# A graph filter layer: its first product in three-part bf16 instead of fp32

## Chip, cores and metric

The kernel runs on one core of one Trainium2 chip. The metric is the time of one execution in device microseconds (us). Three runs of the kernel before took 5813.36, 5824.89 and 5824.14 us, median 5824.14 us.

## What is computed

12,500 nodes have 128 features each; 400,000 edges, sorted by their target, have a source node, a target node, 20 attributes and a weight. The layer is a message passing step with a pre-norm and a residual:

```python
h = jnp.maximum(_layernorm(x), 0.0) @ W_in2f.T
Wij = smu(edge_attr_20 @ W_f1.T + b_f1) @ W_f2.T + b_f2      # per edge
Wij = Wij * edge_weight[:, None]
agg = segment_sum(h[dst] * Wij, src)                          # 12,500 sums
x = x + smu(agg @ W_o1.T + b_o1) @ W_o2.T + b_o2
```

`smu(x)` is close to a gelu: it is computed as `gelu(s x)` plus a multiple of `x`. The names follow the kernel: it gathers `h` by `dst`, in which the edges are sorted, and sums by `src`, which is in no order.

## The kernel before

Edges are taken 128 at a time (a tile), four tiles to a **unit** of 512 edges and two units to a pair; there are 784 units. Every engine runs the same sequence of beats, one unit to a beat, with its own instruction stream written out by `step` functions: some beats are unrolled, most stand in loops of four. In beat n an engine works partly on unit n and partly on unit n-1.

For one unit:

- SP loads, once in two units, the attributes `attr` (20 rows x 1024 edges, fp32, with a row of ones for the bias), the targets `ends` and the window `win` of `h` (L440 to L455).
- PE: `filter1` multiplies the attributes by `w_f1` into `p_z` (L1129, one fp32 product of 128 rows x 512 columns, which the trace shows as two MATMUL records). ACT takes the gelu of it (L678), DVE adds the linear part into `act1` (`smu`, L921).
- PE: `rank` counts for each edge its place among edges of the same bucket (L1152, L1168 into `p_pos`); DVE turns that into row numbers (`places` L945, `row_idx` L956).
- PE: `targets` picks the rows of `h` by a one-hot product (12 bf16 products into `p_h`, L1146: `h` is held in three bf16 parts). ACT weighs them by the edge weight (`hg`, L689). `filter2` (4 fp32 products, 8 records, L1135) gives `p_w`. DVE multiplies the two into `msg` (L938).
- POOL scatters the unit's 512 messages to rows in DRAM with four indirect DMAs (L553), after it has waited for `row_idx`, the keys and `msg`.

The order of PE's beat n is `filter1(n)`, `bucket_sum`, `rank(n-1)`, `targets(n-1)`, `filter2(n-1)`. There is one bank `p_z`, so `filter1(n)` waits for `smu(n-1)`; `targets(n-1)` waits until ACT has emptied `p_h` of the unit before. DVE's beat n is the one-hot of a bucket (`seg_hot`, L971), `smu(n)`, `pick` (L925), `onehot` (L930), `places(n-1)`, the sum into `agg`, `row_idx` and `msg(n-1)`.

The units are done in ten rounds (112, 112, 112, 112, 112, 80, 60, 40, 28, 16 units). From round 1 on the beats also read back the buckets that the round before has scattered (`seg`, L466) and sum them on PE with fp32 products (`bucket_sum`, L1180). Round 0 has none of that; it holds the rest of the layer norm and of `h` and the zeroing of the buckets instead. A prologue before the first beat prepares the first nodes, row numbers and constants. After the last unit come 28 groups of the output layers.

Of the kernel before, what the change touches and what calls it, by code (L numbers as in the profile page):

```python
# [6 lines left out]
ALU = mybir.AluOpType  # L7
# [3 lines left out]
LANES = 128  # L11
TILES_U = 4
UNIT = LANES * TILES_U
# [3 lines left out]
BODY = 4  # L17
DEEP = 7
PARTS = 3
WINDOW = LANES  # L20
# [62 lines left out]
def build(nc, n_nodes, n_edges, n_real, F, R, t):  # L83
# [21 lines left out]
    real_tiles = -(-n_real // LANES)  # L105
    PREPS = 12
# [18 lines left out]
    ends16 = nc.dram_tensor("ends16", [1, n_edges], U16, kind="Internal")  # L125
    reach_dram = nc.dram_tensor("reach_dram", [chunks, CHUNK], F32, kind="Internal")
# [3 lines left out]
    with ctx:  # L130
# [22 lines left out]
        w_f1 = sb("w_f1", [LANES, F])  # L153
        w_f2 = sb("w_f2", [F, F])
# [32 lines left out]
        attr = sb("attr", [LANES, 2, PAIR])  # L187
# [30 lines left out]
        hid_lin = hg[:, :, :, :].rearrange("p b k f -> p b (k f)")[:, :, 0:GROUP]  # L218
        g_dst = sb("g_dst", [LANES, TILES_U], I32)
# [29 lines left out]
        s_limit, s_last = sem("s_limit"), sem("s_last")  # L249
        s_st, s_ag, s_sqrt, s_rstd, s_shift = sem("s_st"), sem("s_ag"), sem("s_sqrt"), sem("s_rstd"), sem("s_shift")  # L250
# [85 lines left out]
        class Beat:  # L336
# [26 lines left out]

            def q(self, back=0):
                return (self.c - back) // 2 % 2
# [41 lines left out]
        def _(sp):  # L407
# [8 lines left out]

            load_x(0)
            sp.dma_start(win_first[:, :], t["dst_first"]).then_inc(s_first, 16)
# [7 lines left out]
            sp.dma_start(w_f1[R:R + 1, :], t["b_f1"]).then_inc(s_ld, 16)  # L426
            for dst, src in ((w_f2[:, :], t["w_f2T"]), (w_o1[:, :], t["w_o1T"]), (w_o2[:, :], t["w_o2T"]),
                             (bias_o1[:, :], t["biases"][0, 1, :].unsqueeze(1)),
                             (bias_o2[:, :], t["biases"][0, 2, :].partition_broadcast(NODE_P))):
                sp.dma_start(dst, src).then_inc(s_ld, 16)  # L430
            for g in range(H_AHEAD):
# [72 lines left out]
            def everywhere():  # L504
                sp.wait_ge(s_z, n_units)
                sp.wait_ge(s_ph, n_units)
                with sp.Fori(0, n_units) as u:
                    sp.wait_ge(g_msg, u)
                    sp.sem_inc(s_carry, 1)
                    sp.dma_start(attr[0:R, 0, 0:UNIT], t["attrT"][:, bass.ds(u * UNIT, UNIT)]).then_inc(g_ld, 16)  # L510
# [9 lines left out]
        def _(pool):  # L520
            pool.memset(w_f1[:, :], 0.0).then_inc(s_pool, 1)
# [789 lines left out]
```

## Time and profile before

| | |
|---|---|
| median of 3 runs | 5824.14 us |
| the profiled execution | 5816.75 us |
| its span, first to last instruction | 5815.0 us |
| mean granted TensorE clock | 0.824 of 2.4 GHz |
| PE, PEld busy | 4372.5, 3583.8 us |
| DVE, ACT, POOL busy | 3423.3, 2117.0, 3038.9 us |
| DMA | 736.96 MB, mean 127 GB/s |

The page gives busy times over the whole span. The kernel has 784 equal beats, so a busy time divided by 784 is that of a beat, and 5815.0 / 784 = 7.42 us is the time there is for one, prologue and end included. In timelines "idle before" stands in square brackets with what ended it; `remote` means that the profile found no instruction of this core whose end fits.

### The profile page before, as it was taken

The numbers are of one execution on the slowest core, as the hardware profiler recorded it, in microseconds if no ns is written. First come the engines' busy times: TensorE is split into PE (matmuls) and PEld (weight loads), VectorE is DVE, ScalarE is ACT, GpSimd is POOL, SyncE is SP. The second block draws the span as 40 slices with busy tenths as digits, with TensorE's granted clock in tenths as the row PEclk, the third lists the DMA queues.
The fourth block names the chain that finished last, engine by engine and source line by source line (L and its number), as shares of the span: only waits on it lengthen the run. The fifth ranks groups of instructions, "written<-read, shape, count | busy, mean of one in ns | idle before, by whom it ended". The sixth has DMA issues, their size and how long they took to land.

```text
span 5815.0 us, 115644 instructions
## 1 busy us (share of the span) xinstructions
PE 4372.5 (75%) x32414; PEld 3583.8 (62%) x32414; DVE 3423.3 (59%) x11901; ACT 2117.0 (36%) x7301; POOL 3038.9 (52%) x3173
## 2 busy tenths in 40 slices
PE   5666557777777777777777777777777788888888
PEld 4455445666666666666666666666666666666667
DVE  5556445555565555555555655555665666666667
ACT  3455333333333333333333333333333333333332
POOL 4555555555555555555555555555555555555552
PEclk7777777877888887888888888888898888888889
DMA  5344334444443333334344434333444444444557
GB/s 161 108 133 135 110 105 131 131 130 130 130 122 113 112 112 115 116 112 115 110 113 115 120 113 114 109 112 117 124 136 134 133 143 142 134 139 145 155 145 196
DMA packets 460268, 736.96 MB, mean 127 GB/s; under 512 B 87920, under 2 KB 256218, under 8 KB 459856
## 3 DMA queue, kind: packets, MB, share of 16 engines
q1 hardware_dynamic: 292886, 461.84, 29.5%
q0 software_dynamic: 100000, 206.60, 10.6%
q10 hardware_dynamic: 67098, 65.08, 3.4%
q8 instruction: 136, 2.23, 0.2%
q14 instruction: 148, 1.21, 0.1%
HBM read 465.36 MB, written 267.82 MB: 126 GB/s over the span
## 4 chain that ended last, share of the span: by engine, by line
another core or an unknown queue 35%; PE 31%; issue 13%; DVE 9%; ACT 8%; ACTq 2%; DMA 1%; DVEq 1%; SPq 0%
PE p_seg L1180 8%; PE p_w L1135 7%; PE p_z L1129 7%; PE p_h L1146 7%; ACT hg L689 4%; DVE product L945 2%; ACT p_w L703 1%; PE p_pos L1152 1%; DVE seg_hot L971 1%; DVE onehot L930 1%; PE p_pos L1168 1%; DVE act L921 1%; ACT gelu L678 1%; ACTq L651 1%
## 5 line engine op out<-in xcount | busy, mean ns | idle before, releaser
L553 POOL DMA_INDIRECT sorted_rows<-msg,row_idx x3125 | 2997.8, 959 | 2685.0 <-DVE msg L938 1759.0
L689 ACT ACTIVATE hg<-p_h,weight 128x128 f32<-128x128 f32 x3136 | 894.6, 369 | 3163.3 <-remote 2888.8
L1180 PEld LDWEIGHTS p_seg<-seg_hot,seg 128*128 128x128 f32 x8288 | 1229.6, 215 | 818.9 <-issue 815.6
L945 DVE CUSTOM_DVE_ANT_0 product<-onehot,p_pos,start_at 128x112 bf16<-128x112 bf16 x3136 | 848.4, 327 | 1419.6 <-remote 1378.6
L1180 PE MATMUL p_seg<-seg_hot,seg 128*128 128x112 f32 x8288 | 1301.9, 300 | 353.9 <-issue 325.1
L1135 PE MATMUL p_w<-w_f,act 128*128 128x128 f32 x6272 | 1148.4, 327 | 238.6 <-issue 235.9
L1129 PE MATMUL p_z<-attr,w_f 128*128 128x512 f32 x1568 | 999.1, 715 | 192.4 <-issue 106.8
L1135 PEld LDWEIGHTS p_w<-w_f,act 128*128 128x128 f32 x6272 | 987.0, 233 | 247.7 <-issue 245.9
L1146 PE MATMUL p_h<-win,pick 128*128 128x128 bf16 x9408 | 831.4, 250 | 297.9 <-ACT hg L689 242.7
L938 DVE TENSOR_TENSOR msg<-p_w,hg 128x512 f32<-128x512 f32 x784 | 541.1, 690 | 757.5 <-ACT hg L689 512.3
L1146 PEld LDWEIGHTS p_h<-win,pick 128*128 128x128 bf16 x9408 | 701.7, 114 | 334.4 <-issue 333.5
L678 ACT ACTIVATE gelu<-p_z 128x512 f32<-128x512 f32 x784 | 474.0, 605 | 409.5 <-PE p_z L1129 160.0
L921 DVE SCALAR_TENSOR_TENSOR act<-p_z,gelu 128x512 f32<-128x512 f32 x784 | 539.0, 688 | 142.7 <-issue 93.2
L971 DVE SCALAR_TENSOR_TENSOR seg_hot<-seg,p_iota 128x560 f32<-128x560 f32 (+3 forms) x756 | 589.9, 787 | 11.2 <-DMA seg<-sorted_rows 7.5
L1152 PE MATMUL p_pos<-onehot,not_before 128*128 128x112 bf16 x3136 | 338.2, 234 | 259.2 <-DVE place L945 137.4
L1152 PEld LDWEIGHTS p_pos<-onehot,not_before 128*128 128x128 bf16 x3136 | 258.4, 111 | 410.4 <-issue 397.3
L930 DVE TENSOR_TENSOR onehot<-p_iota,node_l 128x448 bf16<-128x448 f32 x784 | 482.5, 615 | 0.0
L703 ACT COPY p_w<-bias_f 128x512 f32<-128x512 f32 x784 | 477.8, 609 | 0.0
L1129 PEld LDWEIGHTS p_z<-attr,w_f 128*128 128x128 f32 x1568 | 297.9, 228 | 288.5 <-issue 206.7
L1168 PE MATMUL p_pos<-onehot,before 128*128 128x112 bf16 x3136 | 336.6, 237 | 31.3 <-issue 31.2
L925 DVE TENSOR_SCALAR pick<-ends,win_row 128x512 bf16<-128x512 uint16 x784 | 297.6, 380 | 0.0
L945 DVE DVE_READ_ACCUMULATOR2_ANT place<- 128x1 f32 x3136 | 265.1, 85 | 0.0
(109 smaller groups left out, 1706.7 us busy)
## 6 DMA issues: line engine op xcount, KB each, us to landing
seg<-sorted_rows SPq DMA_DIRECT2D x560, 322.5 KB
ends<-ends SPq DMA_DIRECT2D x392, 256.0 KB
seg<-sorted_rows SPq DMA_DIRECT2D x112, 516.0 KB
sorted_rows<-msg,row_idx POOLq DMA_INDIRECT x3125
sorted_rows<-zero_rows ACTq DMA_DIRECT2D x336, 129.0 KB
win<-h SPq DMA_DIRECT2D x392, 96.0 KB
attr<-in_attrT SPq DMA_DIRECT2D x392, 80.0 KB
seg<-sorted_rows SPq DMA_DIRECT2D x56, 387.0 KB
```

The source lines that it names most:

```text
L553: pool.indirect_dma_start(out=sorted_rows[:, :], out_offset=bass.IndirectOffsetOnAxis(ap=row_idx[:, slot, k:k + 1], axis=0), in_=msg[:, sl ...
L689: last = act.activation(hg[:, v, k, :], p_h[:, k, :], ACT.Copy, scale=weight[:, bass.ds(n.value(TILES_U, k), 1)])
L921: dve.scalar_tensor_tensor(act1[:, v, :], p_z[:, :], SMU_L, gelu[:, v, :], ALU.mult, ALU.add).then_inc(s_smu, 1)
L930: dve.tensor_tensor(onehot[:, slot, :, :], p_iota[:, 0:BUCKETS].unsqueeze(1).to_broadcast([LANES, TILES_U, BUCKETS]), node_l[:, bass.ds(n. ...
L938: dve.tensor_tensor(msg[:, slot, :, 0:F], p_w[v][:, :, :], hg[:, v, :, :], ALU.mult).then_inc(s_msg, 1)
L945: last = dve.tensor_tensor_reduce(out=product[:, k, :], in0=onehot[:, slot, k, :], in1=p_pos[:, 0:BUCKETS], scale=1.0, scalar=start_at[:, ...
L971: dve.scalar_tensor_tensor(seg_hot[:, it.slot, 0:n, :], seg[:, it.slot, 0:n, F:F + 1].to_broadcast([LANES, n, NODE_P]), -float(LANES * (it ...
L1129: pe.matmul(p_z[:, :], w_f1[:, :], attr[:, q, v * UNIT:(v + 1) * UNIT], start=True, stop=True).then_inc(s_z, 1)
L1135: last = pe.matmul(p_w[v][:, k, :], act1[:, v, k * LANES:(k + 1) * LANES], w_f2[:, :], start=False, stop=(k == TILES_U - 1), skip_group_ch ...
L1146: last = pe.matmul(p_h[:, k, :], pick[:, v, k * LANES:(k + 1) * LANES], win[:, q, part * F:(part + 1) * F], start=(part == 0), stop=(part ...
L1152: last = pe.matmul(p_pos[:, 0:BUCKETS], not_before[:, :], onehot[:, slot, k, :], start=False, stop=False, skip_group_check=True)
L1180: last = pe.matmul(out, seg[:, it.slot, l * it.tiles + k, 0:F], seg_hot[:, it.slot, l * it.tiles + k, :], start=(k == 0), stop=(k == it.ti ...
```

## The change

Attributes and first-layer weights (with their bias) are each split into three bf16 parts that add up to the fp32 value. The weights are split once, in the prologue, on DVE, and laid out by 12 small DMAs into `w_z` (128 rows: part 0 three times 20 rows against the three attribute parts, part 1 the same, and the three parts of the bias on rows of ones) and `w_z3` (64 rows: part 2 against the three attribute parts). `filter1` becomes two accumulating bf16 products of 512 columns.

The attributes are split on the chip for each **quad** of four units: SP loads `raw` (80 rows x 512, fp32), ACT casts it (`part_one`), DVE subtracts (`part_rest`), ACT casts the rest (`part_two`), DVE subtracts again (`part_three`), and SP stores the three parts to a DRAM tensor `attr3` in four DMAs. `load_pair` then loads the pair's 60 rows x 1024 bf16 from there twice, into two groups of rows of `attr`. A quad is split two quads ahead of its use.

```diff
-                sp.dma_start(attr[0:R, q, :], t["attrT"][:, bass.ds(p.value() * PAIR, PAIR)]).then_inc(s_attr[q], 16)
+                if p.i is None and p.base % 2 == 0:
+                    sp.wait_ge(s_written, 16 * QUAD * (p.base // 2 + 1))
+                elif p.i is not None and p.base % 2 == 0:
+                    wait_for(sp, s_written, p.over(2), 16 * QUAD, 16 * QUAD)
+                    sp.sem_inc(s_carry, 1)
+                for twin in range(2):
+                    sp.dma_start(attr[twin * PARTS * R:(twin + 1) * PARTS * R, q, :],
+                                 attr3[bass.ds(p.value(PARTS * R), PARTS * R), :]).then_inc(s_attr[q], 16)
...
+            def load_raw(q):
+                wait_for(sp, s_rest, q)
+                sp.sem_inc(s_carry, 1)
+                sp.dma_start(raw[:, :], t["attr_quad"][bass.ds(q.value() * split_rows, split_rows), :]).then_inc(s_raw, 16)
+
+            def store_parts(q):
+                wait_for(sp, s_part3, q, 1, 1)
+                sp.sem_inc(s_carry, 1)
+                for k in range(QUAD):
...
+                    sp.dma_start(rows.rearrange("(a r) e -> r a e", r=R), part[k * R:(k + 1) * R, :, :]).then_inc(s_written, 16)
...
+                if st.quad(1, 1) is not None:
+                    store_parts(st.quad(1, 1))
+                if st.quad(1) is not None:
+                    load_raw(st.quad(1))
...
+            def part_one(q):
+                wait_for(act, s_raw, q, 16, 16)
+                wait_for(act, s_written, q, 16 * QUAD)
+                act.copy(part[:, 0, :], raw[:, :]).then_inc(s_part1, 1)
+
+            def part_two(q):
+                wait_for(act, s_rest, q, 1, 1)
+                act.copy(part[:, 1, :], rest[:, :]).then_inc(s_part2, 1)
...
+                if st.quad(0) is not None:
+                    part_one(st.quad(0))
+                if st.quad(1) is not None:
+                    part_two(st.quad(1))
...
+            def part_rest(q):
+                wait_for(dve, s_part1, q, 1, 1)
+                wait_for(dve, s_part3, q)
+                dve.tensor_tensor(rest[:, :], raw[:, :], part[:, 0, :], ALU.subtract).then_inc(s_rest, 1)
+
+            def part_three(q):
+                wait_for(dve, s_part2, q, 1, 1)
+                dve.tensor_tensor(part[:, 2, :], rest[:, :], part[:, 1, :], ALU.subtract).then_inc(s_part3, 1)
...
+                if st.quad(1) is not None:
+                    part_rest(st.quad(1))
+                if st.quad(2) is not None:
+                    part_three(st.quad(2))
...
-                    wait_for(pe, s_attr[q], p.over(2), 16, 16)
+                    wait_for(pe, s_attr[q], p.over(2), 32, 32)
                 wait_for(pe, s_smu, n)
-                pe.matmul(p_z[:, :], w_f1[:, :], attr[:, q, v * UNIT:(v + 1) * UNIT], start=True, stop=True).then_inc(s_z, 1)
+                cols = slice(v * UNIT, (v + 1) * UNIT)
+                pe.matmul(p_z[:, :], w_z[:, :], attr[:, q, cols], start=True, stop=False)
+                pe.matmul(p_z[:, :], w_z3[:, :], attr[0:LANES // 2, q, cols], start=False, stop=True).then_inc(s_z, 1)
```

`quad(phase)` is true in one beat of four, the one whose number leaves `phase`. The prologue gets the splits of quads 0 and 1, the split of the weights, and a wait of PE for `s_wz`.

How the streams change. **DVE**, an unrolled beat of a round with bucket sums in the kernel before, around `msg` and `smu` (the rows of `places` left out at both ends; `s_hg`, `s_w` are the ends of ACT's weighing and of `filter2`):

```order
L956 TENSOR_TENSOR row_idx<-place,place_max 128x4 [waits s_scat1,s_place]
L938 TENSOR_TENSOR msg<-p_w,hg 128x4x128 [waits s_scat1,s_w,s_hg]
L971 SCALAR_TENSOR_TENSOR seg_hot<-seg,p_iota 128x560 [waits s_seg,s_segld0]
L921 SCALAR_TENSOR_TENSOR act<-p_z,gelu 128x512 [waits s_w,s_gelu]
L925 TENSOR_SCALAR pick<-ends,win_row 128x512 [waits s_ph]
L930 TENSOR_TENSOR onehot<-p_iota,node_l 128x448 [waits s_rank]
```

and the same place with the change, in a beat that splits:

```order
L1054 TENSOR_TENSOR row_idx<-place,place_max 128x4 [waits s_scat0,s_place]
L1036 TENSOR_TENSOR msg<-p_w,hg 128x4x128 [waits s_scat0,s_w,s_hg]
L1069 SCALAR_TENSOR_TENSOR seg_hot<-seg,p_iota 128x560 [waits s_seg,s_segld1,s_ends1]
L963 TENSOR_TENSOR part<-rest,part 80x512 [waits s_part2]
L1019 SCALAR_TENSOR_TENSOR act<-p_z,gelu 128x512 [waits s_w,s_gelu]
L1023 TENSOR_SCALAR pick<-ends,win_row 128x512 [waits s_ph]
L1028 TENSOR_TENSOR onehot<-p_iota,node_l 128x448 [waits s_rank]
```

The subtraction stands between a message and the next `smu`, never ahead of the message itself; in the beat before it L959 stands at the same place.

**SP**, one quad of the steady part with the change (`attr` in rows L453 is the DRAM tensor `attr3`):

```order
L521 DMA seg<-sorted_rows 128x645 [waits s_seg] x2
L453 DMA attr<-part 20x3x512 [waits s_part3]
L453 DMA attr<-part 20x3x512 x3
L445 DMA raw<-in_attr_quad 80x512 [waits s_rest]
L521 DMA seg<-sorted_rows 128x645 [waits s_seg]
L495 DMA attr<-attr 60x1024 [waits s_z]
L495 DMA attr<-attr 60x1024
L501 DMA ends<-ends 128x1024 [waits s_pick]
```

Before, the three `seg` loads, one `attr` load and the `ends` load followed each other; four stores, `raw` and a second `attr` load are put between them.

**PE**, end of the prologue, before:

```order
L1106 MATMUL p_seg<-w_in,hT 128x128 x3
L1122 MATMUL p_w<-bias_f,ident 128x128 [waits s_seeds,s_pool,s_pool2,s_scaled]
L1122 MATMUL p_w<-bias_f,ident 128x128 x7
L1129 MATMUL p_z<-attr,w_f 128x512 [waits s_attr0]
L1129 MATMUL p_z<-attr,w_f 128x512 [waits s_smu]
```

and with the change:

```order
L1209 MATMUL p_seg<-w_in,hT 128x128 x3
L1226 MATMUL p_w<-bias_f,ident 128x128 [waits s_pool,s_seeds,s_wz,s_pool2,s_scaled]
L1226 MATMUL p_w<-bias_f,ident 128x128 x7
L1234 MATMUL p_z<-attr,w_z 128x512 [waits s_attr0]
L1235 MATMUL p_z<-attr,w_z 128x512
L1234 MATMUL p_z<-attr,w_z 128x512 [waits s_smu]
L1235 MATMUL p_z<-attr,w_z 128x512
```

PE's first products now also wait for the laid-out weights, and `p_z` takes two instructions.

## Rows read from the trace of the kernel before

**Rows 1.** Page, part 5: line engine op out<-in xcount | busy, mean ns | idle before, releaser.
```profile
L553 POOL DMA_INDIRECT sorted_rows<-msg,row_idx x3125 | 2997.8, 959 | 2685.0 <-DVE msg L938 1759.0
L689 ACT ACTIVATE hg<-p_h,weight 128x128 f32<-128x128 f32 x3136 | 894.6, 369 | 3163.3 <-remote 2888.8
L1129 PE MATMUL p_z<-attr,w_f 128*128 128x512 f32 x1568 | 999.1, 715 | 192.4 <-issue 106.8
```
**Rows 2.** Busy time by stretch: late round 0, round 1 and 2, rounds 6 and 7.
```profile
core 0: us, PE busy (x) PEld busy (x) DVE busy (x) ACT busy (x) POOL busy (x), PEclk, DMA share, GB/s
620.00:800.00 180.00, 107.79 (x772) 82.32 (x770) 86.37 (x329) 65.01 (x228) 96.82 (x101) 0.74 0.36 107
1000.00:1600.00 600.00, 462.39 (x3301) 376.33 (x3302) 341.72 (x1194) 213.49 (x755) 314.86 (x329) 0.80 0.44 130
4700.00:5300.00 600.00, 489.37 (x3791) 410.90 (x3790) 372.68 (x1257) 212.19 (x753) 320.85 (x334) 0.87 0.47 139
```
**Rows 3.** Timeline, 2021 to 2038 us, some rows: start, us, instruction [idle before <-releaser].
```profile
2021.04 0.96 POOL L553 DMA_INDIRECT sorted_rows<-msg,row_idx  x1 [0.31 <-issue]
...
2023.63 0.33 DVE L945 CUSTOM_DVE_ANT_0 product<-onehot,p_pos,start_at 128x112 bf16<-128x112 bf16 x1 [6.00 <-remote]
2023.94 1.14 ACT L689 ACTIVATE hg<-p_h,weight 128x128 f32<-128x128 f32 x4 [7.92 <-remote]
...
2025.12 0.69 DVE L938 TENSOR_TENSOR msg<-p_w,hg 128x512 f32<-128x512 f32 x1
...
2025.33 0.61 ACT L703 COPY p_w<-bias_f 128x512 f32<-128x512 f32 x1
...
2025.73 0.73 DVE L971 SCALAR_TENSOR_TENSOR seg_hot<-seg,p_iota 128x560 f32<-128x560 f32 x1
2025.85 0.62 ACT L678 ACTIVATE gelu<-p_z 128x512 f32<-128x512 f32 x1
2026.50 0.69 DVE L921 SCALAR_TENSOR_TENSOR act<-p_z,gelu 128x512 f32<-128x512 f32 x1
2026.71 0.96 POOL L553 DMA_INDIRECT sorted_rows<-msg,row_idx  x1 [4.72 <-DVE msg L938]
...
2028.57 1.02 PE L1129 MATMUL p_z<-attr,w_f 128*128 128x512 f32 x2
...
2029.24 0.69 DVE L938 TENSOR_TENSOR msg<-p_w,hg 128x512 f32<-128x512 f32 x1
2029.43 1.26 PE L1180 MATMUL p_seg<-seg_hot,seg 128*128 128x112 f32 x10
...
2030.93 0.83 PE L1146 MATMUL p_h<-win,pick 128*128 128x128 bf16 x12
...
2035.55 0.96 POOL L553 DMA_INDIRECT sorted_rows<-msg,row_idx  x1 [0.30 <-issue]
...
2038.31 1.14 ACT L689 ACTIVATE hg<-p_h,weight 128x128 f32<-128x128 f32 x4 [8.08 <-remote]
```
**Rows 4.** Timeline near the end of round 9, where POOL has run dry.
```profile
5690.24 0.83 PE L1146 MATMUL p_h<-win,pick 128*128 128x128 bf16 x12
...
5691.12 1.14 ACT L689 ACTIVATE hg<-p_h,weight 128x128 f32<-128x128 f32 x4 [3.91 <-PE p_h L1146]
...
5694.46 0.83 PE L1146 MATMUL p_h<-win,pick 128*128 128x128 bf16 x12
...
5695.33 1.14 ACT L689 ACTIVATE hg<-p_h,weight 128x128 f32<-128x128 f32 x4 [2.22 <-PE p_h L1146]
```
**Rows 5.** Timeline of the prologue.
```profile
21.43 0.22 DVE L897 TENSOR_SCALAR w_f<-w_f 128x128 f32<-128x128 f32 x1
...
29.25 0.69 DVE L834 TENSOR_TENSOR h_parts<-h_rest,h_parts 128x512 bf16<-128x512 f32 x1 [0.68 <-ACT h_parts L642]
...
30.59 3.75 PE L1122 MATMUL p_w<-bias_f,ident 128*128 128x128 f32 x16 [3.37 <-DVE seeds L905]
```
**Rows 6.** POOL alone, a unit that is scattered alone.
```profile
3021.56 0.96 POOL L553 DMA_INDIRECT sorted_rows<-msg,row_idx  x1 [0.30 <-issue]
3025.16 0.96 POOL L553 DMA_INDIRECT sorted_rows<-msg,row_idx  x1 [2.64 <-DVE msg L938]
```

More of the change, by code:

```diff
@@ L19 @@
 PARTS = 3
+QUAD = 4
+LEAD = 2
 WINDOW = LANES
@@ L105, in build @@
     real_tiles = -(-n_real // LANES)
+    n_quads = n_units // QUAD
+    assert n_units % QUAD == 0 and 2 * PARTS * R + PARTS <= LANES
+    split_rows = QUAD * R
     PREPS = 12
@@ L153, in build @@
         w_f1 = sb("w_f1", [LANES, F])
+        w_rest = sb("w_rest", [R + 1, F])
+        w_part = sb("w_part", [R + 1, PARTS, F], BF16)
+        w_z = sb("w_z", [LANES, F], BF16)
+        w_z3 = sb("w_z3", [LANES // 2, F], BF16)
         w_f2 = sb("w_f2", [F, F])
@@ L185, in build @@
         counts = sb("counts", [1, rounds + 1, BUCKETS])
-        attr = sb("attr", [LANES, 2, PAIR])
+        attr = sb("attr", [LANES, 2, PAIR], BF16)
+        raw = sb("raw", [split_rows, UNIT])
+        rest = sb("rest", [split_rows, UNIT])
+        part = sb("part", [split_rows, PARTS, UNIT], BF16)
         ends = sb("ends", [LANES, 2, PAIR], U16)
@@ L218, in build @@
         hid_lin = hg[:, :, :, :].rearrange("p b k f -> p b (k f)")[:, :, 0:GROUP]
+        g_attr = gelu[:, 1, :]
         g_dst = sb("g_dst", [LANES, TILES_U], I32)
@@ L249, in build @@
         s_limit, s_last = sem("s_limit"), sem("s_last")
+        s_raw, s_part1, s_rest, s_part2, s_part3, s_w3 = (
+            sem(n) for n in ("s_raw", "s_part1", "s_rest", "s_part2", "s_part3", "s_w3"))
+        s_written = sem("s_written")
+        s_wz, s_wpart, s_wzero = sem("s_wz"), sem("s_wpart"), sem("s_wzero")
         s_st, s_ag, s_sqrt, s_rstd, s_shift = sem("s_st"), sem("s_ag"), sem("s_sqrt"), sem("s_rstd"), sem("s_shift")
@@ L362, in chunk, with quad @@
                 return self.first(back) // CHUNK if self.i is None and self.has(back) and self.first(back) % CHUNK == 0 else None
+            def quad(self, phase, back=0):
+                if self.c % QUAD != phase or self.rnd >= rounds:
+                    return None
+                at = Count((starts[self.rnd] + self.c) // QUAD + LEAD - back, BODY // QUAD if self.i is not None else 0, self.i)
+                return at if self.i is not None or at.base < n_quads else None
             def q(self, back=0):
@@ L430, in _ @@
                 sp.dma_start(dst, src).then_inc(s_ld, 16)
+            sp.wait_ge(s_wpart, 1)
+            sp.wait_ge(s_wzero, 1)
+            for k in range(2 * PARTS):
+                sp.dma_start(w_z[k * R:(k + 1) * R, :], w_part[0:R, k // PARTS, :]).then_inc(s_wz, 16)
+            for k in range(PARTS):
+                sp.dma_start(w_z3[k * R:(k + 1) * R, :], w_part[0:R, 2, :]).then_inc(s_wz, 16)
+                sp.dma_start(w_z[2 * PARTS * R + k:2 * PARTS * R + k + 1, :], w_part[R:R + 1, k, :]).then_inc(s_wz, 16)
+            store_parts(Count(0))
             for g in range(H_AHEAD):
@@ L894, in _ @@
             dve.wait_ge(s_ld, 16 * N_LD)
+            part_three(Count(0))
+            dve.tensor_copy(w_rest[:, :], w_f1[0:R + 1, :]).then_inc(s_w3, 1)
+            dve.wait_ge(s_w3, 1)
+            for k in range(PARTS - 1):
+                link(dve.tensor_copy(w_part[:, k, :], w_rest[:, :]))
+                link(dve.tensor_tensor(w_rest[:, :], w_rest[:, :], w_part[:, k, :], ALU.subtract))
+            dve.tensor_copy(w_part[:, PARTS - 1, :], w_rest[:, :]).then_inc(s_wpart, 1)
             dve.tensor_scalar(bias_gelu[:, :], bias_o1[:, :], SMU_S, None, ALU.mult)
@@ L901, in _ @@
                 third_part(g)
+            part_rest(Count(1))
+            part_three(Count(1))
             dve.wait_ge(s_pool, 4)
@@ L1231, in everywhere @@
                     pe.wait_ge(g_ld, u * 32 + 32)
-                    pe.matmul(p_z[:, :], w_f1[:, :], attr[:, 0, 0:UNIT], start=True, stop=True).then_inc(g_z, 1)
+                    pe.matmul(p_z[:, :], w_f1[:, :], g_attr[:, :], start=True, stop=True).then_inc(g_z, 1)
                     pe.wait_ge(g_win, u * (16 * TILES_U) + 16 * TILES_U)
```

18 lines of the change are left out of this document (17 added, 1 removed).

## The prediction

> **What bounds the kernel now.** I read the page's costliest groups first. They mislead: PE is busy 75% of the span, yet two idle times are larger than any work. ACT waits 2888.8 us for `remote` ahead of weighing `p_h`, and POOL waits 1759.0 us for messages [rows 1]. A bound by PE would show PE full and the others waiting for it in varying amounts, so I then asked for the pace of the beats in stretches with different PE work. Four scatters make a unit. In late round 0 there are 101 scatters in 180 us, 7.13 us per unit; PE has no bucket sums there and is busy 107.79 / 25.25 = 4.27 us per unit. In rounds 1 and 2 it is 7.29 us per unit with PE at 5.62 us, in rounds 6 and 7 7.19 us with PE at 5.86 us [rows 2]. So 1.35 to 1.59 us more PE work per unit costs 0.06 to 0.16 us, and DVE's work grows in the same stretches (3.42, 4.15, 4.46 us) as freely. Traffic of 107, 130 or 139 GB/s makes no difference either. Only POOL is the same everywhere.
>
> The timeline says how [rows 3]. POOL works in bursts of eight scatters, 1.26 us apart (0.96 busy, 0.30 issue), 10.1 us in all. While such a burst runs, PE's ends come late: the 12 products into `p_h` are recorded at 2030.93 for 0.83 us, but ACT, which needs nothing else, weighs them only at 2038.31, for `remote`. The last scatter of that burst ended at 2035.55 + 0.96 = 2036.51, 1.8 us earlier. One cycle back it is the same: last scatter until 2022.00, DVE goes on at 2023.63 and ACT at 2023.94. Where POOL has run dry, `p_h` of 5690.24 is weighed at 5691.12 and that of 5694.46 at 5695.33, right after its end, and the beat takes 4.2 us though it has 32 bucket records [rows 4]. What holds PE's ends back I can't see; that they come free 1.6 to 1.9 us after a burst I can. From that the cycle follows: release at 2023.9, `hg` 1.14 us, `msg` 0.69 us until 2025.81, POOL 0.90 us later at 2026.71; the second unit's message is ready before the first unit's four scatters are done, so POOL runs eight; release again. 10.1 + 1.8 + 2.8 = 14.7 us less 0.3 us of the last issue gap, 14.4 us for two units, 7.2 us each.
>
> **PE's part of the change.** Removed: 784 fp32 products of 512 columns. A record is 715 ns in the mean and busy time is 999.1 us [rows 1]; back to back the pair holds the array for 2029.43 - 2028.57 = 0.86 us at the full clock [rows 3]. Added: two bf16 products of 512 columns. The 12 of 128 columns into `p_h` take 0.83 us, of which the last one's drain is a good part, so 0.05 to 0.07 us each [rows 3]; four times the columns are 0.22 to 0.28 us, 0.43 to 0.55 us for the pair. The array is relieved of 0.3 to 0.4 us per unit at 2.4 GHz, up to twice that at 1.2 GHz: 240 to 630 us in all. On the path I cost it at **0**. `filter1(n)` ends inside the stretch in which nothing that PE ends is seen, or ahead of it; its cover is POOL's burst. The message that starts a burst hangs on the `p_h` and `p_w` of the unit before, which stand ahead of the next `filter1` in PE's order. The slope of rows 2 gives the other end: 0.16 us per 1.35 us, times 0.4 to 0.8 us, times 784, is -37 to -74 us.
>
> The Trainium skill, "FP8 and Floating Point Precision", section "TensorE Precision Notes", says that a true fp32 product takes four passes of the array. By that rule this product falls from four passes to two; the trace agrees (0.86 us against two times 0.22 us), and a kernel whose path ran through PE would gain that. It is the first rival below that it would make true.
>
> **DVE and ACT.** Added per quad: two subtractions of 80 x 512 fp32. `smu`, of the same width, takes 0.69 us [rows 3]; so 1.38 us per quad. ACT: two casts of 80 x 512, like the copy of 0.61 us [rows 3]. Both lie between a message and the next `smu`; the message that starts POOL is not behind them. The second message of a burst is: after the release DVE goes `msg`, `seg_hot` until 2026.46, `smu` at 2026.50, and ACT the copy until 2025.94, `gelu` until 2026.47. A cast (0.61) and then a subtraction (0.69), with `gelu` beside the latter, move this `smu` by 0.7 us and the message of 2029.24 with it. It ended at 2029.93 and POOL needs it at 2026.71 + 4 x 1.26 - 0.90 = 30.85 on this scale, so there is **0.9 us of slack**. Each quad has two such beats, and where a split falls into the other beat of a cycle it lies in the wait. Mostly the slack holds; I allow one cycle in four a loss of 0.1 us or so, 392 / 4 x 0.1 = **10 us**. Bounds: nothing, and 0.7 us in every second cycle, 137 us.
>
> **SP and DMA.** Per quad SP issues 1 raw load, 4 stores and 2 more attribute loads, 7 DMAs. SP is three beats ahead of the others, and every new wait (`s_part3`, `s_rest`, `s_written`) is for work of a beat that lies at least two back, so **0**. Queued behind them are `seg`, `ends` and `win`, for beats later. Bytes: 160 + 240 + 480 KB instead of 160 KB per quad, 720 KB x 196 = 141 MB, 19% more than 737 MB. Rows 2 show the same pace from 107 to 139 GB/s: **0**. The other end: if a quad's 720 KB stood on the path at some 300 GB/s, 2.4 us x 196 = 470 us.
>
> **Prologue.** DVE gets two subtractions ahead of the first `h` parts (1.4 us), the split of the weights, six small operations that wait for each other (0.22 us each as the scaling at 21.43, with the waits about 1.5 us), and the split of quad 1 (two more subtractions with ACT's casts between, 2.6 us) between its last `h_parts` at 29.25 and the `seeds` for which PE's `p_w` products of 30.59 wait [rows 5]. SP's 12 small DMAs and 4 stores run beside that. About **+5 us**, bounds 2 and 12. The end of the kernel is not touched.
>
> **Sum** on the profiled execution: 5816.75 - 0 + 10 + 0 + 5 = 5832. The median of the runs is 7.4 us above that execution, so 5839; I say **5838 us**, +0.24%. A measurement of this kernel tells about 0.2%, 11.6 us, from no change.
>
> **Rivals.** *A, PE's work counts (the other side).* The late ends could be PE's own backlog: it works through products that are queued, and the coincidence with POOL follows from POOL waiting for PE. Then 0.43 us per unit, 337 us, give 5490; at half that share, with the cycle partly POOL's, 5660; by the slope of rows 2 5750 to 5790. Against: rounds without bucket sums are no faster. It decides from the point where a third unit passes PE before the ends are held, or where the first message comes earlier. For a small gain, something speaks: the cold clock after a release (the clock is 0.74 to 0.87 in rows 2, so part of the time at 1.2 GHz) makes that beat's products slow.
>
> *B, the split costs a burst.* If the second message comes after POOL's fourth scatter by more than a moment, PE's ends of the unit behind are caught too and POOL scatters four alone. Such a unit is seen: its last scatter starts at 3021.56 and the next burst at 3025.16, 5.05 + 2.3 = 7.4 us for one unit instead of 7.2 [rows 6]. In half the cycles, that is 0.2 x 392 = 78 us; with the 0.7 us delays on top, 5824 + 78 + 70 = 5970. It decides where the slack is under 0.7 us.
>
> *C, the change does not arrive:* the attributes make a round trip through DRAM, and if stores or the second load are late, `filter1` waits for `s_attr` once a quad. At 1 us, 5824 + 196 = 6020. Against: two quads of lead.
>
> **How the numbers follow.** The forecast, pace unchanged with 2 to 30 us of small costs, has 0.50; with the rounding of measurement half of it lies within 0.2%, half above. A has 0.30, mostly its small form. B has 0.15, C 0.05. So faster 0.29, same 0.28, slower 0.43. The range: 5740, the slope's gain, to 5920, most of B; about 0.1 is left out on each side.
>
> **What would show it.** Right: POOL's scatters still in eights with 4.6 us between, `remote` ahead of `hg` still near 2900 us, PE's busy time down by 400 us or more, pace of rows 2 unchanged, first `gelu` 5 us later. Wrong: `remote` falls by hundreds of us with PE's busy time (A), more bursts of four (B), or PE waits for DMA ahead of `p_z` (C).

## The result, and the profile after

| | before | changed |
|---|---|---|
| median of the runs | 5822.62 us (4) | 5874.93 us (4) |
| the profiled execution, its span | 5816.75, 5815.0 us | 5860.67, 5858.8 us |
| ratio | | 1.0092, 95% interval 1.0078 to 1.0105 |
| PE, DVE, ACT, POOL busy | 4372.5, 3423.3, 2117.0, 3038.9 us | 4302.2, 3659.3, 2307.9, 3118.8 us |
| granted clock, mean | 0.824 | 0.797 |
| DMA | 736.96 MB | 881.68 MB |

The change costs 52 us, 0.9%. I had forecast a loss of 14 us. The page's groups, to be held against [rows 1] (line, engine, op, out<-in, count | busy, mean ns | idle before, releaser):

```profile
L615 POOL DMA_INDIRECT sorted_rows<-msg,row_idx x3125 | 3077.5, 985 | 2650.2 <-DVE msg L1036 1718.9
L764 ACT ACTIVATE hg<-p_h,weight 128x128 f32<-128x128 f32 x3136 | 896.0, 369 | 3182.4 <-remote 2833.0
L1286 PE MATMUL p_seg<-seg_hot,seg 128*128 128x112 f32 x8288 | 1415.0, 320 | 339.8 <-issue 318.1
...
L1234 PE MATMUL p_z<-attr,w_z 128*128 128x512 bf16 x784 | 348.3, 444 | 234.6 <-issue 137.0
...
L1235 PE MATMUL p_z<-attr,w_z 64*128 64x512 bf16 x784 | 343.1, 438 | 84.1 <-issue 82.7
```

The first filter's group fell by 308 us (999.1 to 348.3 + 343.1), and nothing of it arrived. POOL's 3125 scatters are the same instructions with the same bytes, yet they take 79.7 us more. The three stretches of [rows 2] in the changed kernel:

```profile
core 0: us, PE busy (x) PEld busy (x) DVE busy (x) ACT busy (x) POOL busy (x), PEclk, DMA share, GB/s
620.00:800.00 180.00, 102.59 (x758) 79.94 (x759) 93.17 (x340) 69.60 (x238) 100.27 (x101) 0.70 0.47 131
1000.00:1600.00 600.00, 445.43 (x3295) 364.84 (x3292) 362.27 (x1227) 228.15 (x778) 326.98 (x330) 0.79 0.54 155
4700.00:5300.00 600.00, 472.24 (x3710) 397.05 (x3710) 392.95 (x1283) 228.80 (x779) 323.73 (x331) 0.83 0.56 163
```

The number of scatters per stretch is as before (101, 330, 331 against 101, 329, 334), but POOL's busy time for each scatter is up, by 3.6, 3.5 and 1.8%. So the pace nearly holds and the scatters themselves grew. The timeline shows how, in the place that answers to [rows 3]:

```profile
2012.52 0.69 DVE L1036 TENSOR_TENSOR msg<-p_w,hg 128x512 f32<-128x512 f32 x1
...
2013.13 0.73 DVE L1069 SCALAR_TENSOR_TENSOR seg_hot<-seg,p_iota 128x560 f32<-128x560 f32 x1
2014.00 0.69 DVE L959 TENSOR_TENSOR rest<-raw,part 80x512 f32<-80x512 f32 x1
2014.12 1.55 POOL L615 DMA_INDIRECT sorted_rows<-msg,row_idx  x1 [4.79 <-DVE msg L1036]
...
2015.97 0.96 POOL L615 DMA_INDIRECT sorted_rows<-msg,row_idx  x1 [0.30 <-issue]
...
2028.83 0.96 POOL L615 DMA_INDIRECT sorted_rows<-msg,row_idx  x1 [4.32 <-DVE msg L1036]
```

The scatter begins 0.12 us after the new subtraction, which ends at 2014.69; it takes 1.55 us, that is the 0.57 us until then plus its usual 0.96. The next one and the first of the next burst take 0.96 again. There are 176 scatters of 1100 ns and more, against 7 before.

From here on I divide every span along POOL, since it is the engine that all of them follow. The rows are sums over its 3125 scatters and the times between them, in us; gaps under 0.6 us are issue gaps, longer ones are waits.

| profiled execution | to first scatter | scatters | issue gaps | waits | after the last | span |
|---|---|---|---|---|---|---|
| before | 45.9 | 2997.8 | 813.5 | 1831.5 | 126.3 | 5815.0 |
| changed | 56.4 | 3077.5 | 816.3 | 1783.8 | 124.8 | 5858.8 |
| before_again | 47.6 | 2998.6 | 814.4 | 1840.2 | 123.8 | 5824.6 |
| after_again | 60.2 | 3078.0 | 817.5 | 1778.5 | 126.3 | 5860.3 |
| split_alone | 56.3 | 3078.3 | 822.7 | 1772.4 | 126.3 | 5855.9 |
| *other chips:* no_split | 55.1 | 3000.3 | 952.0 | 13.2 | 124.6 | 4145.1 |
| before_psum | 48.1 | 3012.8 | 951.7 | 8.0 | 124.1 | 4144.8 |
| before_port_b | 47.6 | 3053.0 | 951.1 | 13.4 | 123.9 | 4189.0 |
| pool_delay | 45.3 | 3006.7 | 892.6 | 133.0 | 124.1 | 4201.5 |
| one_input_b | 55.9 | 3017.3 | 950.6 | 21.7 | 123.7 | 4169.3 |
| after_c | 57.1 | 3051.5 | 951.7 | 17.0 | 125.3 | 4202.7 |
| late | 56.4 | 3052.6 | 947.9 | 33.0 | 125.0 | 4214.9 |

Changed less before: +10.5 for the start, +79.7 for the scatters, +2.8 issue, -47.7 waits, -1.5 at the end: 43.8 us, the whole difference of the two spans.

**Two kinds of chip.** The experiments met four chips. On one the kernel before takes 5822 us as above; on the three others 4137.46, 4138.23 and 4137.51 us. Which chip the result itself was measured on isn't known; its 5822.62 us put it with the first kind. Whether it is the chip that differs, or something else that came with it, no run shows. A number is only compared with the kernel before as timed beside it on the same chip; on the 4138 us chips the kernel before was timed and not profiled. What differs is in the table's fifth column: on the other three POOL hardly ever waits (8 to 33 us; the 133 us of pool_delay hold its own added work). The `hg` group of after_c there, and the timeline of before_port_b:

```profile
L764 ACT ACTIVATE hg<-p_h,weight 128x128 f32<-128x128 f32 x3136 | 891.6, 367 | 662.3 <-PE p_h L1252 618.5
```
```profile
2094.67 0.95 POOL L556 DMA_INDIRECT sorted_rows<-msg,row_idx  x1 [0.30 <-issue]
...
2095.49 0.83 PE L1153 MATMUL p_h<-win,pick 128*128 128x128 bf16 x12
...
2096.55 1.14 ACT L692 ACTIVATE hg<-p_h,weight 128x128 f32<-128x128 f32 x4 [0.44 <-PE p_h L1153]
2097.19 0.96 POOL L556 DMA_INDIRECT sorted_rows<-msg,row_idx  x1 [0.30 <-issue]
```

Here `hg` follows its products by 0.23 us in the middle of unbroken scatters, where [rows 3] had it wait 6.6 us for `remote`. These chips are the plainer instrument: every us on POOL is a us of the kernel, 3125 x (0.96 + 0.305) us = 3953 of 4138.

### The profile page after: what moved, and what is told of

The parts are those of the page before. It is cut to its first block, busy times and chain, and to the rows that moved or that the text cites. A ratio compares the mean times of both kernels' runs of the same rounds, so it can differ in the third digit from the quotient of the medians.

```text
span 5858.8 us, 120689 instructions
## 1 busy us (share of the span) xinstructions
PE 4302.2 (73%) x32414; PEld 3541.6 (60%) x32414; DVE 3659.3 (62%) x12299; ACT 2307.9 (39%) x7693; POOL 3118.8 (53%) x3175
## 2 busy tenths in 40 slices
DMA packets 581381, 881.68 MB, mean 150 GB/s; under 512 B 107102, under 2 KB 322440, under 8 KB 580958
## 3 DMA queue, kind: packets, MB, share of 16 engines
q0 software_dynamic: 100000, 206.60, 10.5%
## 4 chain that ended last, share of the span: by engine, by line
another core or an unknown queue 31%; PE 31%; issue 14%; ACT 12%; DVE 6%; ACTq 2%; DMA 1%; SPq 0%; DVEq 0%
PE p_seg L1286 10%; PE p_h L1252 7%; PE p_w L1241 7%; ACT hg L764 4%; PE p_z L1235 2%; ACT p_w L778 2%; PE p_z L1234 2%; ACT gelu L753 2%; PE p_pos L1258 1%; DVE product L1043 1%; PE p_pos L1274 1%; ACTq L713 1%; DVE seg_hot L1069 1%; DVE onehot L1028 1%
## 5 line engine op out<-in xcount | busy, mean ns | idle before, releaser
L615 POOL DMA_INDIRECT sorted_rows<-msg,row_idx x3125 | 3077.5, 985 | 2650.2 <-DVE msg L1036 1718.9
L1286 PE MATMUL p_seg<-seg_hot,seg 128*128 128x112 f32 x8288 | 1415.0, 320 | 339.8 <-issue 318.1
L1241 PE MATMUL p_w<-w_f,act 128*128 128x128 f32 x6272 | 1177.2, 336 | 211.9 <-issue 208.6
L1241 PEld LDWEIGHTS p_w<-w_f,act 128*128 128x128 f32 x6272 | 1022.3, 242 | 215.1 <-issue 213.5
L1252 PE MATMUL p_h<-win,pick 128*128 128x128 bf16 x9408 | 870.6, 258 | 284.8 <-ACT hg L764 248.6
L1252 PEld LDWEIGHTS p_h<-win,pick 128*128 128x128 bf16 x9408 | 741.4, 119 | 318.3 <-issue 317.5
L1019 DVE SCALAR_TENSOR_TENSOR act<-p_z,gelu 128x512 f32<-128x512 f32 x784 | 534.7, 682 | 93.6 <-issue 69.3
L1234 PE MATMUL p_z<-attr,w_z 128*128 128x512 bf16 x784 | 348.3, 444 | 234.6 <-issue 137.0
L1235 PE MATMUL p_z<-attr,w_z 64*128 64x512 bf16 x784 | 343.1, 438 | 84.1 <-issue 82.7
L1274 PE MATMUL p_pos<-onehot,before 128*128 128x112 bf16 x3136 | 351.5, 244 | 62.4 <-issue 62.3
L1235 PEld LDWEIGHTS p_z<-attr,w_z 64*128 64x128 bf16 x784 | 73.9, 94 | 387.5 <-issue 387.5
L1023 DVE TENSOR_SCALAR pick<-ends,win_row 128x512 bf16<-128x512 uint16 x784 | 295.0, 376 | 0.0
```

Of the source, the lines that this page charges most:

```text
L615: pool.indirect_dma_start(out=sorted_rows[:, :], out_offset=bass.IndirectOffsetOnAxis(ap=row_idx[:, slot, k:k + 1], axis=0), in_=msg[:, sl ...
L1241: last = pe.matmul(p_w[v][:, k, :], act1[:, v, k * LANES:(k + 1) * LANES], w_f2[:, :], start=False, stop=(k == TILES_U - 1), skip_group_ch ...
L1252: last = pe.matmul(p_h[:, k, :], pick[:, v, k * LANES:(k + 1) * LANES], win[:, q, part * F:(part + 1) * F], start=(part == 0), stop=(part ...
L1286: last = pe.matmul(out, seg[:, it.slot, l * it.tiles + k, 0:F], seg_hot[:, it.slot, l * it.tiles + k, :], start=(k == 0), stop=(k == it.ti ...
```

## The experiments

The theories: **port** (a scatter that begins while DVE reads two operands from SBUF is held until it ends), with the start-up beside it; against **TensorE** (the product's relief or its clock), **bytes** (145 MB more) and **slack** (DVE's added time makes the messages late).

**On the kind of chip of the result.** The two kernels again, and the changed one with the fp32 product and the loads of before, which splits and stores without anybody reading it:

```diff
-                for twin in range(2):
-                    sp.dma_start(attr[twin * PARTS * R:(twin + 1) * PARTS * R, q, :],
-                                 attr3[bass.ds(p.value(PARTS * R), PARTS * R), :]).then_inc(s_attr[q], 16)
+                sp.dma_start(attr[0:R, q, :], t["attrT"][:, bass.ds(p.value() * PAIR, PAIR)]).then_inc(s_attr[q], 16)
...
-                pe.matmul(p_z[:, :], w_z[:, :], attr[:, q, cols], start=True, stop=False)
-                pe.matmul(p_z[:, :], w_z3[:, :], attr[0:LANES // 2, q, cols], start=False, stop=True).then_inc(s_z, 1)
+                pe.matmul(p_z[:, :], w_f1[:, :], attr[:, q, cols], start=True, stop=True).then_inc(s_z, 1)
```

> The kernel before, for a profile of it on the chip of the experiments: 4137 us, scatters of 959 ns as on the first chip (busy 2998 us), none of the waits that the first chip's trace put down as remote, start-up as on the first chip (first gelu at 37 us).

> The changed kernel itself on the chip of the experiments, where the kernel before takes 4137 us and not 5823 us. There GpSimd waits for a message only 78 us in all beside its issue gaps, so its busy time is the time: the port theory expects busy near 3078 us as on the first chip and the kernel at +80 +8 us, about 4225 us (ratio 1.021). If the 48 us that GpSimd waited less on the first chip come back here too, 4180 us. TensorE theory (two bf16 products instead of one fp32 product are the gain): not above 4137 us.

> The changed kernel with the fp32 product and the attribute loads of before; it still splits and stores the parts, which nobody reads back. Port theory: the same as the changed kernel within 10 us, with long scatters as many. Bytes theory: some 60% of the added cost, since of the added 145 MB the stores and the quad loads stay and the double loads are gone. TensorE theory: slower than the changed kernel by 100 us and more, since the first filter's product is back at 715 ns a piece of four passes.

Measured: these runs met the 5822 us chip, so the numbers that were expected for the other kind of chip weren't tried by it. Before 5822.09 us; after_again 5863.12 us, 1.0081 [1.0067, 1.0095]; split_alone 5853.94 us, 1.0055 [1.0042, 1.0069]. The groups of split_alone:

```profile
L609 POOL DMA_INDIRECT sorted_rows<-msg,row_idx x3125 | 3078.3, 985 | 2645.1 <-DVE msg L1030 1714.3
L1228 PE MATMUL p_z<-attr,w_f 128*128 128x512 f32 x1568 | 989.8, 707 | 249.8 <-issue 168.6
```

The heavy product is back, 989.8 against 350.3 + 344.8 us in after_again, and the kernel is no slower; it is 9 us faster, with one load where there were two. So TensorE's relief gains nothing here, and the split with its start-up carries 32 of the 41 us. What the other 9 us belong to, the second load or the two-part product, isn't separated. The long scatters are all there (173 of 1100 ns and more), and so is the shorter wait (1772.4), which therefore doesn't come from the lighter product.

**The hold, alone.** The kernel before with two subtractions per quad that nobody waits for; then the same with the second operand in PSUM:

```diff
+                if st.has() and st.c % 4 in (1, 2):
+                    dve.tensor_tensor(rest[:, st.c % 4 - 1, :], raw[:, :], part[:, :], ALU.subtract)
```
```diff
+                if st.has() and st.c % 4 in (1, 2):
+                    dve.tensor_tensor(rest[:, st.c % 4 - 1, :], raw[:, :], p_iota[0:4 * R, :], ALU.subtract)
```

> The kernel before with two VectorE subtractions per quad added, of the changed kernel's size and types (80 x 512, fp32 minus bf16, both operands in SBUF), at the same place in the beat, that nobody waits for. No transfer, no ScalarE work, no TensorE work is changed. Port theory: the long first scatters appear here too, some 160 to 200 of them, GpSimd's busy time rises by 70 to 90 us and the kernel by 30 to 80 us over the one before. Bytes theory: no change (within 10 us). Slack theory: also slower, but with scatters of their old length and more GpSimd idle time.

> The kernel before with two VectorE subtractions per quad, both operands in SBUF, that nobody waits for, a second time; it may meet the other chip. Port theory: some 130 to 180 scatters that begin while one of these subtractions runs take 1100 ns and more, GpSimd's busy time is 55 to 80 us above 2998. Where GpSimd never waits (4137 us chip) that is the whole cost, +46 us as before; where it stands idle between bursts (5822 us chip) part of it comes back, as it did in the changed kernel: +20 to +45 us.

> The same two subtractions, their second operand in PSUM (fp32) instead of SBUF (bf16). Port theory: none of the scatters that begin beside them is held (mean 957 to 970 ns), GpSimd's busy time at most 20 us above 2998, the kernel at +0 to +20 us. If it is not the port but VectorE's time that costs: the same time as with both operands in SBUF, within 5 us.

Measured, all on 4138 us chips: before_port 4183.47 us, 1.0112 [1.0096, 1.0127]; before_port_b 4185.97 us, 1.0115 [1.0099, 1.013]; before_psum 4150.18 us, 1.0032 [1.002, 1.0044]. Timelines of before_port_b and before_psum, the same place in the beat:

```profile
2107.21 0.68 DVE L999 TENSOR_TENSOR rest<-raw,part 80x512 f32<-80x512 f32 x1
2107.30 1.42 POOL L556 DMA_INDIRECT sorted_rows<-msg,row_idx  x1 [0.30 <-issue]
```
```profile
2087.84 0.68 DVE L998 TENSOR_TENSOR rest<-raw,p_iota 80x512 f32<-80x512 f32 x1
2087.95 0.96 POOL L555 DMA_INDIRECT sorted_rows<-msg,row_idx  x1 [0.30 <-issue]
```

Same engine, size, duration and offset (0.09 and 0.11 us); one scatter is held, the other isn't. Scatters sorted by what DVE was executing 0.1 us after they began (count, mean ns, of them over 1050 ns; the smaller groups are left out):

| DVE at that moment | inputs | count | mean | long |
|---|---|---|---|---|
| changed kernel: `rest` L959 | two SBUF | 140 | 1373 | 117 |
| changed kernel: third part L963 | two SBUF | 143 | 1105 | 57 |
| changed kernel: `smu` L1019 | SBUF, PSUM | 401 | 962 | 6 |
| changed kernel: `pick` L1023 | one SBUF, 16-bit in and out | 146 | 974 | 8 |
| changed kernel: `product`, `onehot`, `seg_hot`, `msg`, `agg` | SBUF, PSUM | 424, 317, 161, 149, 75 | 958 or 959 | 0 |
| changed kernel: nothing | | 989 | 958 | 0 |
| before_port_b: subtraction | two SBUF | 180 | 1222 | 138 |
| before_psum: subtraction | SBUF, PSUM | 192 | 959 | 1 |
| before_psum: `pick` L929 | one SBUF, 16-bit in and out | 186 | 1018 | 62 |

Which of the two begins first decides. Of the scatters that begin 0.05 to 0.4 us after a subtraction with two SBUF operands every one is over 1050 ns: 162 of 162 in the changed kernel, 114 of 114 in before_port_b, 97 of 97 in after_c. With the PSUM operand it is 1 of 120 in before_psum and 1 of 102 in one_input_b. Of the 100 in the changed kernel that begin up to 0.1 us ahead of the subtraction none is; 82 of them are among the 143 beside the third part, whence the low share there. The two versions of the subtraction also differ in the type of the second operand (bf16 in SBUF, fp32 in PSUM). A bf16 operand from SBUF alone doesn't hold a scatter: `product` reads bf16 `onehot` from SBUF beside `p_pos` in PSUM, and none of its 424 is long. Two fp32 operands in SBUF weren't tried.

The Trainium skill, "SBUF — State Buffer", section "Who interferes with whom", has this rule: a DVE instruction with two SBUF inputs contends with a GpSimd instruction that reads SBUF, one with at most one outside the 2-port modes doesn't, and `tensor_scalar` can be in such a mode. The table agrees in each line, `pick`'s too, if the scatter is taken for an instruction that reads SBUF. The DVE instructions of 0.6 us and more that stand in every beat of the kernel before take one operand from PSUM (`p_iota`, `p_z`, `p_w`), and only 7 of its scatters reach 1100 ns; six of these stand beside index operations that are done seven times in all (L852, L854, L872).

Bytes aren't needed for it: no transfer was added here, and 46 to 48 us came. Slack isn't it either: the same DVE time costs 12 us with a PSUM operand. These 12 us look like scatters as well (3012.8 against 3000.3 us in no_split, another kernel on another of these chips): 62 are long beside `pick` there, 18 in no_split. before_port had 150 scatters of 1100 ns and more and POOL some 57 us busier than the kernel before of the first table, where 160 to 200 and 70 to 90 us had been expected; the sizes were too high, the sign and the place right.

**The hold without its cause.** An idle iota on POOL ahead of one unit in four:

```diff
+                if held:
+                    wait_for(pool, s_idle, n.over(4))
+                    pool.sem_inc(s_go, 1)
+                    pool.iota(idle[:, :], pattern=[[1, 392]], base=0, channel_multiplier=0,
+                              allow_small_or_imprecise_dtypes=True).then_inc(s_idle, 1)
```

> The kernel before with one iota of some 0.37 us on GpSimd ahead of the scatters of one unit in four: 196 of them, 73 us, and with their fixed part some 80 to 100 us, at no cost to VectorE or to anything else. It is the hold of the changed kernel without its cause. Where GpSimd never waits, all of it is added: +80 to +100 us. Where it idles between bursts: if a hold ahead of a burst gives TensorE time that the wait after the burst then returns (as the changed kernel's 80 us and its 48 us less idle suggest), +30 to +50 us; if the less idle time came from elsewhere (the lighter product, VectorE's order), +80 us and more here too.

Measured on a 4138 us chip: 4203.28 us, 1.0161 [1.0147, 1.0175].

```profile
L560 POOL DMA_INDIRECT sorted_rows<-msg,row_idx x3125 | 3006.7, 962 | 933.5 <-issue 861.2
```

A gap with an iota takes 0.635 us in the mean in place of 0.305, 65 us for 196 of them; 65 us arrive. I had expected 80 to 100: the iota takes 0.45 us, but it begins 0.01 us after the scatter ahead of it ends, inside what was the issue gap. POOL's delay is paid in full on such a chip. On the 5822 us chip this kernel wasn't run, so what a delay costs there stands on the traces alone, below.

**Parts of the change.** First all but the split within the loop; then the changed kernel with PSUM operands; then with the subtractions moved:

```diff
-                if self.c % QUAD != phase or self.rnd >= rounds:
+                if True:
                     return None
...
-                                 attr3[bass.ds(p.value(PARTS * R), PARTS * R), :]).then_inc(s_attr[q], 16)
+                                 attr3[0:PARTS * R, :]).then_inc(s_attr[q], 16)
```
```diff
-                dve.tensor_tensor(rest[:, :], raw[:, :], part[:, 0, :], ALU.subtract).then_inc(s_rest, 1)
+                dve.tensor_tensor(rest[:, :], raw[:, :], p_iota[0:split_rows, :], ALU.subtract).then_inc(s_rest, 1)
...
-                dve.tensor_tensor(part[:, 2, :], rest[:, :], part[:, 1, :], ALU.subtract).then_inc(s_part3, 1)
+                dve.tensor_tensor(part[:, 2, :], rest[:, :], p_iota[0:split_rows, :], ALU.subtract).then_inc(s_part3, 1)
```
```diff
-                if st.quad(1) is not None:
-                    part_rest(st.quad(1))
-                if st.quad(2) is not None:
-                    part_three(st.quad(2))
                 if st.has():
                     smu(st.at(), st.v())
                     pick_target(st.at(), st.pair(), st.q(), st.v())
                     bucket_of(st.at(), st.ring())
+                if st.quad(1) is not None:
+                    part_rest(st.quad(1))
+                if st.quad(2) is not None:
+                    part_three(st.quad(2))
```

> The two bf16 products and the prologue stay; within the loop nothing is split or stored, and every pair loads the parts of pair 0, so the filter's values are those of the first pair for all edges. Port theory with a lighter TensorE that lets GpSimd idle less: GpSimd busy back at 2998, its idle time still some 48 us lower, start-up +8: about 5785 us, 35 to 40 us under the kernel before. If the smaller idle time of the changed kernel was only the other side of longer scatters: 5822 + 8 = 5830 us. TensorE theory (the first filter's product bounds the beat): at least 300 us under the kernel before.

> The two subtractions of a quad keep their place, order, waits and size but take their second operand from PSUM (p_iota, zeroed), so that each reads SBUF on one side only; the parts' values are then not the attributes'. Port theory: a scatter is held only while VectorE reads two operands from SBUF, so the scatters of 1100 ns and more fall from 176 to near the count before (under 20), GpSimd's busy time falls by about 80 us from 3077.5 to near 2998, and the kernel gains 50 to 80 us on the changed one: 5795 to 5825 us. Bytes theory (the 145 MB of added transfers lengthen the cycle): nothing moves, 5875 us. Slack theory (the added VectorE time makes the messages late): nothing moves either, unless PSUM operands make the subtractions shorter.

> The changed kernel with the subtractions' second operand in PSUM, a second time (the values are then not the attributes'). On the 4138 us chip: 4177 us as before, 20 to 50 us under the changed kernel of the same call. On the 5822 us chip, where GpSimd idles between bursts: GpSimd's busy time falls by 65 to 80 us from 3078; if its idle time comes back with it (from 1780 to 1830 us), 20 to 35 us under the changed kernel, 5830 to 5850; if the idle time stays low, 5790 to 5800, under the kernel before; if the hold has nothing to do with the loss there, 5865 to 5875 us.

> The two subtractions move behind bucket_of, so that they begin while VectorE would wait for the rank product rather than at the head of the beat. Port theory: their overlap with the scatters moves with them; if they then fall into the gap between two bursts GpSimd's busy time falls by up to 80 us and the kernel ends at 5800 to 5840 us, if they still fall on a running burst the long scatters are other ones than the first of four and the time stays within 20 us of 5875. Slack theory (the head of the beat is what delays smu, filter2 and so the message): gain of the whole 10 to 50 us wherever the scatters are. Bytes theory: no change.

> The changed kernel once more; on the chip where GpSimd never waits (before 4138 us) it has not been timed. There, from the parts measured so far: start-up and the rest of the change without the split +9 us, the subtractions' own time with one SBUF operand +12 to +31 us, the hold of the scatters +36 us or, by the 80 us of the first chip, more: 4200 to 4230 us, ratio 1.015 to 1.022, GpSimd busy 3050 to 3078 us. If the less idle time of the first chip is a gain of its own and not only the other side of the hold, below 4190 us. On the 5822 us chip: 5863 to 5875 us again.

Measured, all on 4138 us chips:

| | us | ratio to before |
|---|---|---|
| no_split | 4146.43 | 1.0024 [1.0014, 1.0034] |
| one_input | 4177.04 | 1.0096 [1.0081, 1.0112] |
| one_input_b | 4173.36 | 1.0085 [1.0071, 1.0099] |
| after_c | 4204.54 | 1.0164 [1.015, 1.0178] |
| late | 4210.93 | 1.0178 [1.0164, 1.0192] |

one_input, late and no_split were expected in absolute numbers for the 5822 us chip, which none of these runs met; so the PSUM version wasn't tried there. after_c less one_input_b, side by side on one chip, is 31 us, and 34.2 us is the fall of the scatters' time. In one_input_b a scatter that begins beside the subtraction isn't held:

```profile
3316.05 0.68 DVE L959 TENSOR_TENSOR rest<-raw,p_iota 80x512 f32<-80x512 f32 x1 [0.33 <-ACT part L718]
3316.16 0.95 POOL L615 DMA_INDIRECT sorted_rows<-msg,row_idx  x1 [0.30 <-issue]
```

one_input stays 27 to 31 us above no_split: in one_input_b 17 us are longer scatters, mostly beside `pick` (67 of 172 are over 1050 ns, against 18 of 184), some 9 us waits. no_split has the light product, both loads and the prologue, and is 9 us slower than before, with scatters of 3000.3 us and the first of them 9 us later than in the first table: that is the start-up, and the product's relief gains nothing here either. The move in late helped nothing, its interval overlaps after_c's: 90 of the 99 scatters that begin beside `rest` are held there too. With POOL never idle there is no gap for the subtraction to fall into.

So on these chips the change's 67 us are 9 of start-up, some 27 of added DVE time, and 31 of the subtractions' hold. Even with the split gone altogether the kernel is behind the one before by its start-up. A version with a shorter prologue wasn't tried.

**Why the hold costs less on the 5822 us chip.** 80 us longer scatters and 48 us less wait come together, in after_again (79.4 and 61.7 against before_again) and in split_alone (79.7 and 67.8). Within the one trace of the changed kernel, bursts of eight sorted by whether one of their scatters was held (count; us from the first scatter to the end of the last; wait behind it; sum):

```
held   141   10.29   4.25   14.54
free   173    9.82   4.64   14.46
```

A held burst is 0.47 us longer and the wait behind it 0.39 us shorter; 141 x 0.39 = 55 us. Not all of it need come from the hold: the 61 free bursts that have a subtraction beside them are followed by 4.53 us, the other 112 by 4.70. Nor does it grow with the hold: behind bursts lengthened by 0.2 to 0.35 us the wait is 4.33 us, by 0.5 to 0.65 us 4.32 us. The held scatter is the first of its burst in 120 of the 141, so the burst's other transfers begin later while TensorE goes on; that this is why the wait is shorter is my reading, and no run shows it. Why TensorE's ends come late at all on this chip stays open too, and pool_delay, which would have tested the return there, met the other kind of chip.

## Why the prediction was right, and where it was off

**Right: what bounds it.** The pace didn't follow PE's work, DVE's or the bytes; split_alone and no_split take the product's relief out of the account on both kinds of chip. The step "On the path I cost it at 0" held, and within the 9 us that split_alone leaves open so did SP and DMA at 0: traffic rose to 131 to 163 GB/s in the stretches with the number of scatters nearly unchanged. The size of the relief was too high: I had the bf16 pair at 0.43 to 0.55 us, and in the changed kernel's trace the next product starts 0.62 us after the first of the pair in nearly half of the beats (375 of 784, the commonest distance), 0.30 us of it for the first product, against 0.86 us for the fp32 one. By the rule of passes of the Trainium skill ("FP8 and Floating Point Precision", "TensorE Precision Notes"), four passes for a true fp32 product, the group would have halved; its busy time fell by 31%, so the trace agrees in the direction only. The kernel's time didn't follow, since no path ran through PE. PE's busy time fell by 70 us in all and not by "400 us or more" as the text said one would see: the p_z group gave 308 us, and the others gave back, with the clock at 0.797 for 0.824 (`p_seg` 320 for 300 ns). With the fp32 product in split_alone the clock is 0.824 again, and on the other chips it is 0.932 to 0.945 with the bf16 products and 0.963 to 0.976 with the fp32 one, so the lower clock comes with them.

**Off: the term for DVE and ACT, 10 us.** The step that failed is "the message that starts POOL is not behind them". True of the message, and not of the scatter. I counted what the subtraction delays on its own engine, the slack of the second message, and not what it shares with the next one. The term measured 80 us of longer scatters, of which some 55 us come back behind the bursts (47.7 net of waits in the sum), and the free bursts' waits are 0.06 us longer than before. How the return works stays open, as said. The rows that I took from before don't show it, since the long DVE instructions of its beats take an operand from PSUM and 7 scatters in all reach 1100 ns. Its trace has it in small, and I had missed it: of the 99 scatters that begin beside `pick`, 25 take over 1050 ns. The bounds of 0 and 137 us held it by luck, since they were worked out for another mechanism; the chosen value was wrong. Rival B, though of the right sign, had the wrong mechanism too: 314 bursts of eight and 82 of four, against 317 and 83.

**Off: the prologue, 5 us.** It measured 8 us at the first `gelu` (45.15 against 37.13) and 10.5 us at the first scatter. The missed wait:

```profile
32.38 0.69 DVE L913 TENSOR_TENSOR h_parts<-h_rest,h_parts 128x512 bf16<-128x512 f32 x1 [0.68 <-ACT h_parts L704]
...
35.71 0.62 ACT L718 CAST part<-raw 80x512 bf16<-80x512 f32 x1 [3.37 <-DMA attr<-part]
36.36 0.69 DVE L959 TENSOR_TENSOR rest<-raw,part 80x512 f32<-80x512 f32 x1 [3.29 <-ACT part L718]
...
37.74 0.69 DVE L963 TENSOR_TENSOR part<-rest,part 80x512 bf16<-80x512 f32 x1 [0.68 <-ACT part L722]
38.35 0.27 DVE L1002 COPY p_iota<-iota 128x112 f32<-128x112 f32 x1
```

Quad 1's first cast waits for quad 0's stores, since `part` is one buffer. DVE is free at 33.07 and reaches what follows at 38.35: 5.3 us where I had 2.6. The other 2.5 us come between the first `gelu` and the first scatter: DVE waits 3.27 us for `x_all<-in_x` where it waited 1.46 us before, and a subtraction of 0.67 us follows. The first scatter is then held itself (the subtraction at 56.27, the scatter at 56.36 for 1.57 us), which counts among the scatters.

**Rivals.** A fell: no part of the relief arrives. C fell as a cause: of PE's 234.6 us of idle time ahead of the first `p_z` product the load of `attr` ended 25.1 us, in 11 waits over 196 quads, against 10.3 us before. The range of 5740 to 5920 held 5874.93, but its upper part was there for B. That the 52 us fell inside it is luck: they came by a way that neither the forecast nor a rival describes.

## What to carry to other kernels

When an edit adds a DVE instruction, look at where its operands lie and what GpSimd begins in the next 0.7 us. Here a subtraction with two SBUF inputs held every scatter that started 0.05 to 0.4 us into it until about its end, the 16-bit `tensor_scalar` some; with an operand from PSUM nearly none was held, at the same 0.68 us of DVE time. Compare the mean duration of instructions that the change didn't touch before any wait is explained: 985 against 959 ns pointed to the cause at once. And work that doesn't bound a kernel can be cut by a third for nothing, here 308 of 999 us of products.

## What the runs showed of the hardware that I had not expected

- The kernel before takes 5822 us on one chip and 4138 us on three others. The difference lies in POOL's waits, 1831.5 us against 8 and 13 in the kernels nearest to it (before_psum, no_split), behind ends of TensorE that come late only while a burst runs.
- A held scatter goes on about when the DVE instruction ends. As first of a burst it pays all that is left of it: 0.57 + 0.96 = 1.53 us, 1.55 measured. Within a burst it pays about 0.13 us less: at 2107.30 in before_port_b 0.59 us are left, and 1.42 us measured are 0.46 over 0.96. So it is in the mean: 0.59 us more with 0.57 us left for 80 scatters of the changed kernel that begin 0.10 to 0.15 us into `rest`, 0.44 us more with 0.56 us left for the 21 like them in before_port_b.
- The hold has another side: of the 151 `pick` in before_port_b that begin while a held scatter runs, 121 take 390 to 420 ns; of the 480 that begin beside a scatter of the usual length, 42 do, and most take the usual 340. What decides between the two stays open.
